# Transformer layer pair on one core: first norm, Q/K/V weight split and projection in one stage, output weights split at the attention's end

## What is computed

```python
x = x + attention(layernorm(x))        # 16 heads of 32, causal, softmax
x = x + experts(layernorm(x))          # 32 experts, top 8 of each token
x = x + state_space(layernorm(x))      # 16 heads, chunks of 64
x = x + lut_ffn(layernorm(x))          # weights looked up in a table of 16
def attention(x):
    q, k, v = x @ Wq + bq, x @ Wk + bk, x @ Wv + bv
    return (softmax(causal(q @ k.T * 32 ** -0.5)) @ v) @ Wo + bo
```

## Time and profile before

| | |
|---|---|
| median of 3 runs | 2733.88 us (2729.54, 2733.88, 2734.23) |
| profiled execution | 2730.05 us, of it 2728.5 from the first to the last instruction |
| busy: PE, DVE, ACT, POOL | 2405.0, 1576.5, 968.6, 975.3 us |
| mean granted clock of TensorE | 0.932 of 2.4 GHz |
| norm stage | 3.96 to about 54 us |
| projection | 54.17 to 195.9 us |
| attention | 195.93 to about 662 us |

### The profile page before, as it was taken

The page is one execution under the profiler, slowest core; times in us unless marked ns, Lnnn a source line. Parts: engine busy times, 40 slices in busy tenths (PEclk is TensorE's granted clock), DMA queues, the critical chain, the costliest instruction groups (busy, mean ns, idle before and its releaser), DMA issues. The chain is left out here.

```text
span 2728.5 us, 48628 instructions
## 1 busy us (share of the span) xinstructions
PE 2405.0 (88%) x12838; PEld 1821.6 (67%) x12840; DVE 1576.5 (58%) x3435; ACT 968.6 (35%) x2184; POOL 975.3 (36%) x880
## 2 busy tenths in 40 slices
PE   4979999995756999999999759999979898899997
PEld 3865455553535888888888738887855554688885
DVE  5226566652665555555555466999278786555553
ACT  3113455553134344444444322222255453222211
POOL 3117888884302666666666401111111110000000
PEclk9987999998865999999999979999989999799998
DMA  4459999995453899999998544547499650100001
GB/s 133 130 138 317 340 330 345 341 334 175 92 190 127 225 258 286 252 243 267 259 251 209 83 147 133 175 162 223 135 231 202 156 122 12 35 23 23 23 9 62
DMA packets 263309, 491.18 MB, mean 180 GB/s; under 512 B 31889, under 2 KB 149137, under 8 KB 253458
## 3 DMA queue, kind: packets, MB, share of 16 engines
q1 hardware_dynamic: 197202, 272.17, 33.5%
q0 software_dynamic: 62976, 212.42, 27.4%
q10 hardware_dynamic: 3024, 5.29, 0.6%
HBM read 592.96 MB, written 198.79 MB: 290 GB/s over the span
## 5 line engine op out<-in xcount | busy, mean ns | idle before, releaser
L1216 PE MATMUL m_ps_u<-m_ring,m_xT_hi 128*128 x1280 | 372.1, 352 | 31.9 <-DMA m_ring<-w_split 19.8
L1182 POOL DMA_INDIRECT expert_sum<-x_res,token_of x160 | 253.4, 1584 | 223.8 <-ACT x_res L1284 128.4
L1216 PEld LDWEIGHTS m_ps_u<-m_ring,m_xT_hi 128*128 128x128 f32 x1280 | 237.6, 190 | 37.1 <-issue 36.7
L628 ACT ACTIVATE probs<-ps_c 128x512 f32<-128x512 f32 (+3 forms) x384 | 182.6, 490 | 214.0 <-PE ps_c L561 129.0
L658 DVE TENSOR_REDUCE neg_max<-ps_r 128x1 f32<-128x512 f32 (+3 forms) x256 | 147.7, 590 | 163.5 <-PE ps_r L528 113.1
L1216 PE MATMUL m_ps_u<-m_ring,m_xT_lo 128*128 x640 | 217.6, 340 | 0.0
L1175 POOL DMA_INDIRECT m_xg<-x_rows,token_of x160 | 177.0, 1106 | 103.9 <-issue 99.6
L1339 DVE SCALAR_TENSOR_TENSOR m_h<-m_silu,m_xg,m_ps_u 128x128 f32<-128x128 f32 x160 | 55.7, 348 | 272.0 <-ACT m_silu L1278 186.7
L1652 PE MATMUL s_ps<-s_x_hi,s_w_hi 128*128 128x512 f32 x512 | 200.5, 392 | 1.9 <-POOL s_w_lo L1622 1.9
L1652 PE MATMUL s_ps<-s_x_lo,s_w_hi 128*128 128x512 f32 x512 | 202.2, 395 | 0.0
L528 PE MATMUL ps_r<-k_st,q_st 96*128 96x512 f32 (+3 forms) x384 | 162.6, 430 | 44.3 <-DMA k_st<-k_parts 19.5
(11 more groups left out here) (335 smaller groups left out, 5758.4 us busy)
## 6 DMA issues: line engine op xcount, KB each, us to landing
m_ring<-w_split SPq DMA_DIRECT2D x160, 1536.0 KB
m_ring<-w_split SPq DMA_DIRECT2D x160, 768.0 KB
w_split<-e_gu_parts POOLq DMA_DIRECT2D x32, 1536.0 KB
proj<-s_out SPq DMA_DIRECT2D x32, 1024.0 KB, 3.9
e_raw_gu<-w_experts POOLq DMA_DIRECT2D x32, 768.0 KB
w_split<-e_dn_parts POOLq DMA_DIRECT2D x32, 768.0 KB
e_raw_dn<-w_experts POOLq DMA_DIRECT2D x32, 512.0 KB
q_st<-q_parts SPq DMA_DIRECT2D x32, 256.0 KB, 6.4
```

What stands on the lines that cost most here:

```text
L628: nc.scalar.activation(probs[a][j % RING][:, :width], ps_c[a][:, :width], ACT.Exp, scale=SCALE).then_inc(exp_done, 1)
L1182: pool.indirect_dma_start(acc[j % 2], rows_at(j), y[j % TURNS], None, bounds_check=PADDED - 1, oob_is_err=True, compute_op=ALU.add).then_i ...
L1216: last = nc.tensor.matmul(ps_u[b % 2][:, :W_UP], x[b % 2][:, k, :], ring[:, first + k * GU_ROW:][:, bass.ds(place, W_UP)], start=(n == 0), ...
```

## The change

One function, `norm_and_project`, takes the place of the norm stage and of `project_qkv`.

- `load_tokens` issues the first quarter of x alone; the other three stand in the new stage's SP list, behind and between the weights.
- Weights come in the order q, v, k, four pieces each, through four buffers. POOL splits eight pieces first and the four of k between its first stores.
- PE transposes four tiles, then goes through 12 `UNITS` (the eight q/k steps of the first token group and four tiles of v), and transposes one of the other 12 tiles behind each; then come the remaining 24 steps and 12 tiles of v without transposes.
- DVE takes moments by pairs of tiles, and works by units: moments of a pair (every second unit), normalise the next tile, low part of q/k or v's sum, low part of x. ACT's root for a pair stands behind its copy in every second unit.
- The stage's semaphores are cleared at its end, as the norm stage's were.
- `wo` is no longer split there. It is loaded in the attention, ahead of the last body, and POOL casts and subtracts it in one piece of 128x2048 behind its last body.

The words under which the change goes also name "experts' weights loaded in small rows". No line of the diff touches their loads or stores.

```diff
+def load_quarter(sp, x_in, x_res, q, loaded):
+    quarter = slice(q * TILES // QUARTERS, (q + 1) * TILES // QUARTERS)
+    sp.dma_start(x_res[:, quarter, :], x_in.rearrange("(n p) d -> p n d", p=P)[:, quarter, :]).then_inc(loaded, 16)
...
-                quarter = slice(q * tiles, (q + 1) * tiles)
-                sp.dma_start(x_res[:, quarter, :], x_in.rearrange("(n p) d -> p n d", p=P)[:, quarter, :]).then_inc(loaded, 16)
+            load_quarter(sp, x_in, x_res, 0, x_loaded[0])
...
-        with ExitStack() as inner:
-            x_hi = inner.enter_context(nc.sbuf_tensor("a_x_hi", [P, KD, N_TOK], F32R))
...
-            w_lo = inner.enter_context(nc.sbuf_tensor("w_qkv_lo", [P, KD, 3 * D], F32R))
-            weights = [(w[k * P:(k + 1) * P, m * D:(m + 1) * D], w_hi[:, k, m * D:(m + 1) * D], w_lo[:, k, m * D:(m + 1) * D])
-                       for m in range(3) for k in range(KD)]
-            weights += [(wo[k * P:(k + 1) * P, :], wo_hi[:, k, :], wo_lo[:, k, :]) for k in range(KD)]
-            layernorm_transposed(nc, "a_ln", x_res, x_hi, x_lo, ident, weights, x_loaded)
-            project_qkv(nc, x_hi, x_lo, w_hi, w_lo, b_qk, b_v, qk, v_rows)
-        attend(nc, qk, v_rows, yT, all_sums, w_raw, w_split)
+        attend(nc, qk, v_rows, yT, all_sums, w_raw, w_split, wo, wo_hi, wo_lo)
         output_projection(nc, x_res, yT, all_sums, inv_sums, wo_hi, wo_lo, bo)
-def project_qkv(nc, x_hi, x_lo, w_hi, w_lo, b_qk, b_v, qk, v_rows):
+def norm_and_project(nc, x_in, x_res, x_loaded, ident, w, b_qk, b_v, qk, v_rows):
...
+    SUB = GROUP // P
+    PAIR = 2
+    PAIRS_OF_TILES = TILES // PAIR
+    STAGES = 4
...
     V_EVERY = len(STEPS) // TILES
+    PIECES = [(c, k) for c in (0, 2, 1) for k in range(KD)]
+    UNITS = [unit for n in range(MT) for unit in ([("qk", n)] if n % V_EVERY < V_EVERY - 1 else [("qk", n), ("v", n // V_EVERY)])]
+    assert len(UNITS) == TILES - SUB and BATCH * T == N_TOK
...
-        sem = nc.alloc_semaphore
+        sem = semaphores(ctx, nc)
...
+        @block.sync
+        def _(sp):
+            def load_w(c):
+                for n in range(c * KD, (c + 1) * KD):
+                    col, k = PIECES[n]
+                    if n >= STAGES:
+                        sp.wait_ge(w_lo_done, n - STAGES + 1)
+                    sp.dma_start(stage[n % STAGES][:, :], w[k * P:(k + 1) * P, col * D:(col + 1) * D]).then_inc(w_loaded[n % STAGES], 16)
+            def load_x(q):
+                load_quarter(sp, x_in, x_res, q, x_loaded[q])
+            load_w(0)
+            load_x(1)
+            sp.dma_start(bias[:, :], b_qk).then_inc(bias_loaded, 16)
+            sp.dma_start(bias_v[:, :], b_v.partition_broadcast(P)).then_inc(bias_loaded, 16)
+            load_x(2)
+            load_w(1)
+            load_x(3)
+            load_w(2)
+            for n in range(len(STEPS)):
+                sp.wait_ge(hi_done, n + 1)
+                sp.dma_start(home(n, 0), hi[:, n % BUFS, :].bitcast(F32)).then_inc(hi_stored[n % BUFS], 16)
+            for b in range(BUFS):
+                sp.wait_ge(hi_stored[b], 16 * len(range(b, len(STEPS), BUFS)))
...
+            def split_w(n):
+                pool.wait_ge(w_hi_done, n + 1)
+                nc.gpsimd.tensor_tensor(part_of(w_lo, n), stage[n % STAGES][:, :], part_of(w_hi, n).bitcast(F32), ALU.subtract).then_inc(w_lo_done, 1)
+            for n in range(2 * KD):
+                split_w(n)
+            for n in range(len(STEPS)):
+                pool.wait_ge(lo_done, n + 1)
+                pool.dma_start(home(n, 1), lo[:, n % BUFS, :].bitcast(F32)).then_inc(lo_stored[n % BUFS], 16)
+                if n < KD:
+                    split_w(2 * KD + n)
+            for b in range(BUFS):
...
+                g, m = STEPS[n]
                 if n >= PS:
                     pe.wait_ge(lo_done, n - PS + 1)
-                toks = slice(g * GROUP, (g + 1) * GROUP)
+                if m == 0:
+                    pe.wait_ge(x_lo_done, (g + 1) * SUB)
+                if n == 0:
+                    pe.wait_ge(w_lo_done, KD)
+                if n == MT // 2:
...
+            def values(t):
+                if t == 0:
+                    pe.wait_ge(w_lo_done, 2 * KD)
+                if t >= 2:
...
+                    values(n)
+                turn(SUB + u)
+            for n in range(MT, len(STEPS)):
+                project(n)
                 if n % V_EVERY == V_EVERY - 1:
-                    t = n // V_EVERY
-                    if t >= 2:
-                        pe.wait_ge(v_added, t - 1)
-                    terms = [(k, x, a) for k in range(KD) for x, a in ((x_hi, w_hi), (x_lo, w_hi), (x_hi, w_lo))]
...
+                    values(n // V_EVERY)
...
+            def deviations(p):
+                act.wait_ge(var_done, p + 1)
+                nc.scalar.activation(std[:, pair(p)], var_eps[:, pair(p)], ACT.Sqrt).then_inc(std_done, 1)
+            def high_w(n):
+                act.wait_ge(w_loaded[n % STAGES], 16 * (n // STAGES + 1))
+                nc.scalar.copy(part_of(w_hi, n), stage[n % STAGES][:, :]).then_inc(w_hi_done, 1)
+            def high_x(i):
+                act.wait_ge(transposed, i + 1)
+                nc.scalar.copy(x_hi[:, :, toks(i)], ps_x[i % 2][:, :, :]).then_inc(x_hi_done, 1)
...
+            for p in range(2):
+                deviations(p)
+            for i in range(SUB):
+                high_w(i)
+                high_x(i)
+                if i == 1:
+                    deviations(2)
+            for n in range(KD, 2 * KD):
+                high_w(n)
+            act.wait_ge(bias_loaded, 32)
+            for u, (kind, n) in enumerate(UNITS):
+                if kind == "qk":
+                    high_qk(n)
+                high_x(SUB + u)
+                if u % PAIR == 1 and u // PAIR + 3 < PAIRS_OF_TILES:
+                    deviations(u // PAIR + 3)
+                if 1 <= u <= KD:
+                    high_w(2 * KD + u - 1)
+            for n in range(MT, len(STEPS)):
+                high_qk(n)
...
+            def pair_moments(p):
+                if p % PAIR == 0:
+                    dve.wait_ge(x_loaded[p // PAIR], 16)
+                for i in range(p * PAIR, (p + 1) * PAIR):
...
+            def normalize(i):
+                p = i // PAIR
+                if i % PAIR == 0:
+                    dve.wait_ge(std_done, p + 1)
+                    nc.vector.reciprocal(rstd[:, pair(p)], std[:, pair(p)]).then_inc(rstd_done, 1)
+                    dve.wait_ge(rstd_done, p + 1)
+                if i >= XB:
+                    dve.wait_ge(transposed, i - XB + 1)
+                nc.vector.tensor_scalar(xn[:, i % XB, :], x_res[:, i, :], mv[:, i, 0:1], rstd[:, i:i + 1], ALU.subtract, ALU.mult).then_inc(xn_ready, 1)
...
+            for i in range(SUB + 1):
+                normalize(i)
+                if i > 0:
+                    low_x(i - 1)
+                if i == 1:
+                    pair_moments(2)
+            dve.wait_ge(bias_loaded, 32)
+            for u, (kind, n) in enumerate(UNITS):
+                i = SUB + u
+                if u % PAIR == 0 and u // PAIR + 3 < PAIRS_OF_TILES:
+                    pair_moments(u // PAIR + 3)
+                if i + 1 < TILES:
+                    normalize(i + 1)
+                if kind == "qk":
+                    low_qk(n)
+                else:
+                    add_v(n)
+                low_x(i)
+            for n in range(MT, len(STEPS)):
+                low_qk(n)
                 if n % V_EVERY == V_EVERY - 1:
-                    t = n // V_EVERY
-                    dve.wait_ge(v_product, t + 1)
...
+            pool.wait_ge(wo_loaded, 16)
+            pool.sem_inc(turns_begun, 1)
+            nc.gpsimd.tensor_copy(wo_hi[:, :, :], raw_wo[:, :, :]).then_inc(wo_split, 1)
+            pool.wait_ge(wo_split, 1)
+            pool.sem_inc(turns_begun, 1)
+            nc.gpsimd.tensor_tensor(wo_lo[:, :, :], raw_wo[:, :, :], wo_hi[:, :, :].bitcast(F32), ALU.subtract).then_inc(wo_split, 1)
             for x in range(2):
...
                 body(it, False)
```

131 lines of the change are left out of this document (87 added, 44 removed).

## The result

Two times came from the same chip: 2733.88 us before and **2715.51 us** after, medians of nine runs each (2722.0 to 2741.6 and 2706.6 to 2730.1). The ratio is 0.9942 with a 95% interval of 0.9925 to 0.9958, which is 15.9 us less, 11.5 to 20.5. (The medians themselves are 18.4 us apart.) The forecast was 2708 in 2699 to 2722: sign and range held; the measured gain is a third smaller than the 24.6 us of the sum. The profiled execution of the changed kernel took 2724.37 us (span 2722.9), in the upper half of its nine.

A forecast was written before the change was run, and what follows sets the result against it. The prediction took TensorE's wait behind the DVE-paced norm stage, then TensorE alone in the projection, as the bound. Its terms, -33.2 + 5.4 + 0.5 + 2.0 + 0.7 = -24.6 us on 2732.6, gave 2708, range 2699 to 2722.

The forecast's parts named there:

- the 24.6 us of the sum: Whole kernel: start -33.2, turns +5.4 and +0.5, stalls +2.0, boundary +0.7 us, together 24.6 us faster.
- Start of the projection: First projection matmul at 21.0 us, between 19.5 and 25, instead of 54.17: 33.2 us earlier.
- Turns, slow start, DVE: Projection: twelve transpose turns cost 5.4 us plus 0.5; slow first matmuls unchanged; DVE nearly ties with TensorE, 2.0 us stalls.
- those pieces down as hidden: Projection: casts and splits of weight pieces 8 to 11, done in units 1 to 4, needed in unit 6; no cost.
- Rival 1: Projection: low clock stays through the twelve units, +33.3 us, giving 2741, slower; 5% chance.
- The tail behind the last matmul stays: End of the projection: time from last matmul to attention (187.87 to 195.93) unchanged.
- The 0.7 us that the prediction put to the boundary: End of the new stage: clearing semaphores and an added empty block cost 0.7 us more.
- Output weights: hidden, with 11 us to spare: Attention's end: POOL's 6.6 us cast and subtraction finish about 646.5, TensorE works until 658.1; zero, at worst a microsecond.
- Rival 4: Attention: POOL's 6.6 us at its end show, or waits for k move; 2715; 2% chance.
- Stages behind keep their lengths within 2 us: Stages after the change: sign that the prediction is right if their lengths move by no more than 2 us.
- a late start: Forecast range: first projection matmul as late as 25 us, with three holds and a late quarter of x.
- stalls of DVE: Forecast range: 0 to 6 us of stalls in the projection's units, where DVE nearly ties with TensorE.

The follow-up runs named there:

- the doubling: Changed kernel with output weights split behind the last max_cols, plus each of the 12 turns between units done twice; 2718.30 us, ratio 0.9946 to the kernel before.
- late_stores_sp: Changed kernel with output weights split behind the last max_cols, plus SP instead of POOL issuing the low stores; 2763.99 us, ratio 1.0128 to the kernel before.
- after_bufs4: Changed kernel with four instead of three store buffers, output weights left as they are; 2713.88 us, ratio 0.9937 to the kernel before.
- late_bufs4: Changed kernel with output weights split behind the last max_cols, plus four instead of three store buffers; 2705.21 us, ratio 0.9919 to the kernel before.

## Why the prediction was right, and where it was wrong

**Start of the projection: right.** 20.19 where 21.0 was predicted. Three holds were met ahead of it and in the first unit (1.22, 1.31 and 1.59 us against 0.55), but not all on the chain, and the second quarter of x was not late.

**Turns, slow start, DVE: right.** From first to last matmul 141.3 us where the sum said 141.6 (133.7 + 5.4 + 0.5 + 2.0). A turn costs 0.43 to 0.49 (the doubling; 3.21 less 2.72), not twice that. TensorE lost 0.3 us in all to a normalised tile that was late (3.47 less 3.21); the stall of 1.65 us came from the last piece of k, and the prediction had put those pieces down as hidden. The 2.0 us for stalls fit by luck, as they came from another source. Rival 1 did not come true: a unit of twelve matmuls with its turn took 3.21 us, four transposes 0.60 and eight 1.03. By that rival 33.3 us more would have been seen. The rule of the Trainium skill, TensorE: Matmul & The Clock Gate, Part 4: PE-mode transpose, that the full clock does not engage for transposes, does not fit these turns between matmuls; the measurement decides.

**"The tail behind the last matmul stays": wrong, 5.3 us in the profiled run** (13.4 against 8.06; 18.1 and 10.6 in the repeats; 7.9, 9.2 and 10.7 with four buffers). The prediction read the landing of nothing but the loads. The earlier trace rows have DVE wait 9.9 and 8.8 us for stores in the stage before; TensorE was four banks of PSUM ahead and did not feel it, but a stage that ends at a barrier does, if such a wait falls on its last step. In the kernel before one of 2.54 us fell there too, and was over before the last matmul; the one of 6.75 us was not. The 0.7 us that the prediction put to the boundary lie in the same tail, and no run separates them.

**"Output weights: hidden, with 11 us to spare": wrong.** This is the step that cost most. The cover was sought in when POOL's queue and TensorE end; the prediction's own mechanism, DVE held by a POOL split, was applied to the norm and not here. A row of the kernel before, of its attention, had it (count, busy us, mean ns):

```profile
L669 DVE CAST max_cols<-neg_max 128x8 fp32r<-128x8 f32 x32 | 31.9, 996 | 3.3
```

A cast of 128x8 that takes 0.17 us alone has a mean of 1.0; one that took 1.96 us, for example, stood at 619.21. In the attention of the kernel before no wait of TensorE for `max_cols` is listed all the same: it has the next head's rows to do. In the last body it has not, and the profile after lists one wait, of 4.4 us. When the subtraction meets `max_cols`, it costs 4.4 us of waiting and some 4 of low clock behind it (windows of 22.8 and 19.0 us). With a k load 0.9 us later and a short time at low clock, the last two heads were 11.1 us longer. Rival 4 named the place with 2%, and priced it at 6.6 by the length on POOL's side alone.

**"Stages behind keep their lengths within 2 us": wrong.** The experts take 677.2 and 675.9 us in the two profiles with the old norm stage, and 676.5 to 688.9 in eleven with the new code (late_stores_sp left out), with waits for the ring of weights between 15 and 38 us. Two profiles are too few to say whether this is scatter or an effect; it stays open, and may hold a part of what is missing between the 17.2 and 22.9 us at the attention's end in the two undisturbed profiles and the 16 to 17 of the ratios.

**The sum.** At the attention's start the three profiles of the changed kernel are 21.0, 16.0 and 23.9 us ahead; taking 10 for the one collision in three leaves a mean of 17. The three measurements give 15.9, 17.2 and 16.4 (ratios times the median before). With three profiles this is an estimate and no proof. The forecast of 24.6 is what after_bufs4 and late_bufs4 reach when both accidents are away: 24.8 and 27.1 us ahead where the attention ends. By their ratios they are 17.2 and 22.1 us faster in all. That the range held is in part luck: its width was meant for a late start and for stalls of DVE, which did not come, and it took in two terms put at nothing, the tail and the output weights, that did.

The words on experts' weights in small rows have no line in the change, as the prediction said.

## What to carry to other kernels

A piece of work that is moved under another stage is hidden only if nothing of that stage that shares a resource with it is on the chain: look at who is held, not only at when the queues end. A helper's split on POOL, its cast as well as its subtraction, is best cut into short instructions, or put behind a semaphore that says that DVE's last short operation is done. And where a stage ends at a barrier, its last step has to be free of the waits that the middle of the stage can swallow: look there for buffers that wait for their stores.
